# One turn of a 16-batch attention loop laid anew: the order of work on five engines in an adaLN block with linear attention and eight experts

## The reference, cut to what matters

```
h = layernorm(x) * (1 + ca) + sa
q, k = feature_map(h @ Wq.T + bq), feature_map(h @ Wk.T + bk)    # 16 heads, 8 -> 32 features
v = h @ Wv.T + bv
buf = [k.T @ v, sum(k)]
out = (q @ buf)[..., :-1] / (q @ buf)[..., -1:]
x = x + ga * (out @ Wo.T + bo)
h = layernorm(x) * (1 + cb) + sb
x = x + gb * (W2[e](gelu(W1[e](h) + b1[e])) + b2[e]),  e = argmax(h @ gate_W + gate_b)
```

## Time and profile before

| | us |
|---|---|
| median of 3 runs | 383.06 |
| lowest and highest run | 382.57, 385.99 |
| span of the profiled execution | 360.6 |
| what lies around it (median less span) | 22.5 |
| PE busy | 338.8 (94% of the span) |
| DVE, ACT, POOL busy | 271.2, 265.1, 213.2 |
| first part, to the first block's transpose | 0 to 211.4 |
| second part | 211.4 to 360.6 |

### The profile page before, as it was taken

How to read it: one execution, slowest core, us unless ns; L and a number is a source line. 1 busy time by engine, 2 the same in 40 slices (tenths; PEclk the granted TensorE clock), 3 DMA queues, 4 the chain that set the end, 5 groups by cost and what they waited for, 6 DMA issues and landing times.

```text
span 360.6 us, 13729 instructions
## 1 busy us (share of the span) xinstructions
PE 338.8 (94%) x4823; PEld 263.9 (73%) x4823; DVE 271.2 (75%) x1104; ACT 265.1 (74%) x644; POOL 213.2 (59%) x262
## 2 busy tenths in 40 slices
PE   6899999899988999998999999999999999999994
PEld 5445765566465566646665669999989999999993
DVE  3456997898879789878887978887677676666653
ACT  2688988799878888977888756676656667666761
POOL 3142386776667757857854618846767455545554
PEclk9999999999999999999999999999999999999999
DMA  7174656774566547444432467445657665545410
GB/s 233 50 253 166 210 184 221 259 243 160 177 227 205 176 167 230 163 132 156 153 133 100 149 163 227 142 118 150 194 161 269 209 184 147 147 128 135 137 38 12
DMA packets 40211, 60.47 MB, mean 168 GB/s; under 512 B 5426, under 2 KB 28086, under 8 KB 40016
## 3 DMA queue, kind: packets, MB, share of 16 engines
q1 hardware_dynamic: 33776, 42.54, 39.9%
q0 software_dynamic: 6368, 17.05, 12.5%
HBM read 28.63 MB, written 19.34 MB: 133 GB/s over the span
## 4 chain that ended last, share of the span: by engine, by line
PE 60%; ACT 15%; DMA 10%; DVE 6%; issue 5%; POOL 1%; SPq 1%; DVEq 1%; POOLq 0%; ACTq 0%
PE ps_proj L1350 16%; PE ps_feat L1337 9%; DMA qmix<-qsqs 9%; PE ps_proj L1132 6%; PE ps_den_gate L1337 4%; PE ps_proj L1182 4%; PE ps_kv L1337 4%; ACT qf L627 3%; ACT qvals L606 2%; ACT shared L588 2%; PE ps_kv L1198 2%; PE ps_out L1330 2%; ACT den L656 2%; ACT shared L581 2%; ACT kvm L600 2%
## 5 line engine op out<-in xcount | busy, mean ns | idle before, releaser
L545 POOL DMA_INDIRECT out<-kf,modb x71 | 70.1, 987 | 52.4 <-DVE kf L1060 47.0
L507 POOL DMA_INDIRECT experts_lists<-pay,slot x64 | 65.9, 1030 | 43.4 <-DVE slot L893 29.5
L1350 PE MATMUL ps_proj<-w2sb,qf 128*128 x568 | 75.0, 275 | 0.4 <-ACT qf L690 0.4
L1350 PEld LDWEIGHTS ps_proj<-w2sb,qf 128*128 128x128 f32 x568 | 68.9, 192 | 0.6 <-issue 0.6
L681 ACT ACTIVATE xT<-ps_out 128x128 f32<-128x128 f32 x71 | 19.7, 277 | 44.8 <-PE ps_out L1330 44.1
L1055 DVE TENSOR_TENSOR kf<-ps_proj,firsts_sb 128x128 f32<-128x128 f32 x71 | 20.7, 291 | 34.6 <-PE ps_proj L1350 22.6
L690 ACT ACTIVATE qf<-ps_feat,shared 128x128 f32<-128x128 f32 x144 | 40.9, 374 | 0.0
L1337 PE MATMUL ps_feat<-xT,shared 128*128 128x128 f32 x288 | 38.8, 277 | 1.5 <-issue 0.9
L1337 PEld LDWEIGHTS ps_feat<-xT,shared 128*128 128x128 f32 x288 | 35.0, 192 | 2.8 <-issue 1.7
L1132 PE MATMUL ps_proj<-shared,wsb 128*128 128x512 f32 x62 | 33.3, 620 | 1.0 <-ACT shared L581 0.4
L977 DVE COPY shared<-firsts_sb 128x516 f32 x71 | 31.4, 442 | 1.6 <-issue 1.5
(11 more groups left out here) (189 smaller groups left out, 890.3 us busy)
## 6 DMA issues: line engine op xcount, KB each, us to landing
modb<-experts_lists SPq DMA_DIRECT2D x71, 196.0 KB, 2.8
xall<-in_x SPq DMA_DIRECT2D x16, 256.0 KB, 3.0
pay<-modb SPq DMA_DIRECT2D x16, 256.0 KB, 3.0
qmix<-qvals SPq DMA_DIRECT2D x30, 128.0 KB
qmix<-qsqs SPq DMA_DIRECT2D x30, 128.0 KB
modb<-modulation_rows SPq DMA_DIRECT2D x4, 768.0 KB, 5.2
firsts_sb<-in_firsts SPq DMA_DIRECT2D x8, 322.0 KB, 4.2
w2sb<-in_w SPq DMA_DIRECT2D x8, 256.0 KB
```

The lines of the kernel that those rows point to most:

```text
L507: g_.indirect_dma_start(out=lists, in_=pay[b.home][:, t, :], in_offset=None, out_offset=bass.IndirectOffsetOnAxis(ap=slot[b.home][:, t:t + ...
L545: g_.indirect_dma_start(out=rows_out, in_=yb[u], in_offset=None, out_offset=bass.IndirectOffsetOnAxis(ap=token, axis=0), bounds_check=last ...
L1350: ins = mm(Y[u % 2][:, 0:D], g[u % R4][:, c * P:(c + 1) * P], w2sb[:, bass.ds(e * DFF + c * D, D)], start=(c == 0), stop=(c == FC - 1))
```

## The change

The arithmetic is the same; no instruction is added or taken away in a full turn, only order, banks and waits change. Part by part:

- project_k(b+1) stands in PE's turn right behind out_project(b-1) and writes bank G (the bank of the denominator) instead of PJ[0]; it waits until attention(b-1) has read G. k_values and k_squares of b+1 move forward with it on ACT.
- transpose_xn(b+1) stands ahead of out_project(b-1), modulate(b+1) between the two k_pairs, and project_v(b+1) and v_values(b+1) are done in turn b instead of b+1.
- normalise1(b+2) is done by DVE in turn b, behind kv_values, instead of normalise1(b+1) at the turn's head; POOL's rstd1_of goes ahead of rstd2_of.
- ACT makes q_squares(b+1) ahead of the logarithm of batch b instead of behind it.
- On PE gate and gate_transpose go behind kv_product, rank between denominator and numerator.
- On DVE centre_h2(b-1) goes ahead of kv_values(b), slots(b-2) behind scale_h2(b-1), directly ahead of attention(b).
- The single semaphore of the projections becomes three, and the first and the last turn have functions of their own.

```
 # POOL
+                if ahead and b.par == 0:
+                    rstd1_of(b.half + 3, b=b + 2)
                 if not first:
                     rstd2_of(b + -1, rows_of=None if second else b + -2)
-                if ahead and b.par == 0:
-                    rstd1_of(b.half + 3, b=b + 2)
                 if not first and not second:
                     scatter(b + -2, (0, 1))
                 gated(b, first)
 # ACT, the new turn
+                k_pair(b, 0)
+                modulate(b + 1)
+                k_pair(b, 1)
+                if not second:
+                    h2T_copy(b + -2)
+                k_values(b + 1)
+                k_squares(b + 1)
+                q_pair(b, 0)
+                if not second:
+                    gateT(b + -2)
+                q_pair(b, 1)
+                kvm_copy(b)
+                v_values(b + 1)
+                q_values(b + 1)
+                q_squares(b + 1)
+                rden_first(b)
                 if b.v + 2 < B:
                     normalise1(b + 2)
 # DVE
-                if not first and not last:
-                    normalise1(b + 1, lo=LT // 2)
                 if not first:
                     residual(b + -1)
                     second_stats(b + -1)
+                if not first and not last:
+                    centre_h2(b + -1)
...
+                kv_values(b, first)
...
+                if b.v + 2 < B:
+                    normalise1(b + 2, lo=LT // 2)
+                if not first and not second and not last:
                     experts(b + -2)
...
                 eps_values(b)
                 if not first and not last:
-                    centre_h2(b + -1)
                     scale_h2(b + -1)
+                if not first and not second and not last:
+                    slots(b + -2)
 # PE, the new turn
+                k_features(b)
+                if not second:
+                    transpose_h2(b + -2, first=b.v == 2)
+                transpose_xn(b + 1)
+                out_project(b + -1)
+                project_k(b + 1)
+                q_features(b)
+                kv_product(b)
+                if not second:
+                    gate(b + -2)
+                project_v(b + 1)
+                kv_transpose(b)
+                if not second:
+                    gate_transpose(b + -2)
+                project_q(b + 1)
+                eps_and_den(b)
+                if not second:
+                    rank(b + -2, first=b.v == 2)
+                numerator(b)
```

More of the change, by code:

```diff
@@ L277, in build @@
         s_bo = sem("bo_row_ready")
[L278 removed]
+        s_pk = sem("k_projected")
+        s_pq = sem("q_projected")
+        s_pv = sem("v_projected")
         s_kst = sem("k_parts")
@@ L635, in gateT, with rden_first @@
                 a.activation(lgT[:], I[:, 0:P], ACT.Copy).then_inc(s_lgT, 1)
[L637 to L653 removed]
+            def rden_first(b):
                 act.wait_ge(s_den, b.v + 1)
@@ L1278, in batch @@
             def batch(b, first=False, second=False, last=False, ahead=True):
-                third = b.v == 2
+                if first:
+                    return first_batch(b)
                 if last:
-                    count(0)
-                k_features(b, first)
-                if not first and not second:
-                    transpose_h2(b + -2, first=third)
-                v_project(b, last)
-                if not first:
-                    out_project(b + -1)
-                if not first and not second:
+                    return last_batch(b)
@@ L1289, in batch @@
+                k_features(b)
+                if not second:
+                    transpose_h2(b + -2, first=b.v == 2)
+                transpose_xn(b + 1)
+                out_project(b + -1)
+                project_k(b + 1)
+                q_features(b)
+                kv_product(b)
+                if not second:
                     gate(b + -2)
-                q_features(b, first)
-                if not first and not second:
+                project_v(b + 1)
+                kv_transpose(b)
@@ L1292, in batch @@
+                if not second:
                     gate_transpose(b + -2)
-                if not last:
-                    transpose_xn(b + 1)
-                else:
-                    table_transpose(0)
-                kv_product(b, first)
-                if not last:
-                    project(b + 1, 0)
-                if not first and not second and not last:
-                    rank(b + -2, first=third)
-                if last:
-                    keep_busy(10, H)
-                kv_transpose(b, first)
@@ L1305, in batch @@
-                if not last:
-                    project(b + 1, 1)
-                else:
-                    keep_busy(14, H)
-                attend(b)
-                if last:
-                    rank(b + -2)
+                project_q(b + 1)
+                eps_and_den(b)
+                if not second:
+                    rank(b + -2, first=b.v == 2)
+                numerator(b)
             pe.wait_ge(s_fw, 3)
@@ L1318, in _ @@
             mm(KV[0:B, 0:3 * D], sc, wmod_sb[:, 0:3 * D], start=True, stop=True)
-            project(start, 0, first=True)
-            project(start, 1, first=True, bank=I)
+            project_k(start)
+            project_q(start, bank=I)
             mm(G[0:B, 0:3 * D], sc, wmod_sb[:, 3 * D:6 * D], start=True, stop=True).then_inc(s_modp, 1)
```

157 lines of the change are left out of this document (96 added, 61 removed).

## The result

The changed kernel takes 401.74 us (median of 4 runs, 399.65 to 406.74), the kernel before beside it 384.52 (382.57 to 386.57): ratio 1.0453, interval 1.038 to 1.0527. Slower, as forecast; 399 was named, in a range of 388 to 405. One of the four runs, the one of 406.74, shows a lower granted clock than the others (0.973 against 0.980 to 0.986), and the ratio leaves it out. The profiled execution has a span of 400.4 and its own time is 402.22, so 1.8 us lie around its span, and not the 22.5 that the prediction added.

What follows compares the result with a forecast made beforehand. The kernel before was taken as bound by PE plus a DMA wait, the changed one by POOL's scatters and wo. 360.6 + 14.3 + 1.0 + 1.0 = 376.9 us of span, with 22.5 around it 399; range 388 to 405.

Steps and rivals of the forecast that it cites:

- the DMA wait: PE's q_features waiting for the DMA interleaving q's squares: counted as gone, 5.2 us over eight turns, some 8 over the loop.
- odd turn: Loop: slots ends at 9.67, then two scatters and wo end last, so a turn takes 13.02 us instead of 12.5.
- even turn: Turns 4, 6, 8, 10, 12: experts waits behind normalise1 for POOL's late rstd1_of, 1.50 us more, 14.52 in all.
- start: Batch 0: denominator and logarithm come later, out_project(0) by 1.3 us, 0.3 regained in turn 1: +1.0, between 0 and 1.5.
- end and second part: SP's first block load waits for batch 12's later last scatter: +1.0 us, between -0.8 and +1.8; second part unchanged.
- around the span: Outside the profiled execution: 22.5 us added to take the span to the runs' median.
- rival D: Loop: a further wait, scatters slower beside attention or a clock fall to 1.2 GHz; 405 us and more; chance 0.05.
- the clock holds: PE in the loop: despite idling 1.2 us in odd and 2.7 in even turns, the granted clock is not halved.
- port rule: POOL's scatters beside DVE: by the skill page an estimated 5 us more per turn, by the rows nothing; rows' price kept.
- A: Loop: POOL's path does not decide, PE and DVE up to oT do; turns of 11.9, ending at 375.5 us; chance 0.09.
- B: Loop: rstd1_of comes in time, so even turns equal odd ones, 13 turns of 13.02; 392 us; chance 0.12.
- E: Loop: POOL takes what the DMA wait gives, so turns stay 12.5; 383 to 385 us; chance 0.04.

Runs made afterwards that it cites:

- normalise1 late: The changed kernel with DVE's half of normalise1 of two batches on moved behind experts and the epsilon copy: 380.17 us, ratio 1.0505.
- two moves: The changed kernel with gated ahead of the first two scatters on POOL and, in even turns, normalise1's half behind slots on DVE: 378.5 us, ratio 1.0469.
- the squares moved: The kernel before with the squares of q ahead of the logarithm on ACT: 388.93 us, ratio 1.0145.
- slots late: The kernel before with slots behind scale_h2 on DVE, directly ahead of attention: 409.5 us, ratio 1.0708.
- four moves: The changed kernel with gated ahead of the scatters, slots ahead of scale_h2, even-turn normalise1 half behind slots, PE's gate ahead of kv_product: 413.12 us, ratio 1.0799.
- slots early: The changed kernel with slots ahead of scale_h2 on DVE: 373.3 us, ratio 1.0276.
- rstd2_of first: The changed kernel with gated ahead of the scatters, even-turn normalise1 half behind slots, and rstd2_of back ahead of rstd1_of on POOL: 366.0 us, ratio 1.0088.
- gated first: The changed kernel with gated (wo and the bias sum) ahead of the first two scatters on POOL: 373.43 us, ratio 1.0279.

## Why the prediction was right, and where it was not

**Direction and mechanism: right.** POOL's path from slots over two scatters to wo ends last, the DMA wait is gone (it came back in two turns each of the versions with gated and with slots moved, 0.75 to 2.37 us) and pays nothing, even turns are longer for the late shift. That holds in every full turn on chip 1. On chip 2, where the times of the result come from, wo ends last in 7 of the 13 turns alone. On chip 1, where the rows came from, the span was forecast as 376.9 and is 376.9. That agreement is partly luck, as the terms show (from the four windows):

| term | forecast | measured on chip 1 |
|---|---|---|
| odd turn | 13.02 | 12.6 to 12.7 (turn 9: 13.1; turn 14: 13.17) |
| even turn | 14.52 | 14.18 to 14.23 |
| loop, 13 turns | +14.3 | +10.4 |
| start | +1.0 | +1.2 |
| end and second part | +1.0 | +3.4 (in other traces of this order +1.5 to +1.6) and +1.1 |
| around the span | 22.5 | 1.8 |

*The odd turn* (turn 5). The gate's transpose was read at 5.87 (forecast 5.89), experts took 1.23 (1.22, though the two times named beside it, 118.58 to 119.89, are 1.31 apart). scale_h2 stands 1.06 in front of slots, not 1.30: the 1.30 was read from one turn in which it ran beside POOL's work, as did the 1.34 of its busy time; alone it has 1.14. From the end of slots to wo are 2.68, not 2.83, and from there to out_project 0.61, not 0.52. Together 0.34 less in this turn and 3.7 less over the thirteen (173.1 against 176.8). In turns 9 and 14 the first scatter starts 0.76 behind slots instead of 0.29; why, is open.

*The even turn.* The factors are there at 6.83 (forecast 6.80), experts begins at 7.38 (7.39; the terms written out, 6.80 and 0.53, give 7.33, and 0.06 goes unnamed). The 1.50 between the two kinds of turn came out as 1.5. This was the boldest number in the forecast and the best, for it was walked out on POOL instruction by instruction.

*The end* was undersized for this trace. The last scatter of batch 12 starts 3.12 behind out_project(14), as forecast (3.2). SP's next write of gate rows waits until that scatter has landed, and it stands ahead of the first block's load in both kernels; it comes 4.71 behind the scatter, where the kernel before has 2.59. I had kept the same 3.5 for both. That scatter on POOL and the two issues of SP, kernel before and then changed kernel, chip 1:

```profile
203.98 0.96 POOL L507 DMA_INDIRECT experts_lists<-pay,slot  x1 [0.30 <-issue]
...
206.57 0.62 SPq L381 DMA_DIRECT2D pay<-modb  x1
208.88 9.21 SPq L432 DMA_DIRECT2D modb<-experts_lists  x9
```

```profile
217.09 0.96 POOL L516 DMA_INDIRECT experts_lists<-pay,slot  x1 [0.30 <-issue]
...
221.80 0.62 SPq L386 DMA_DIRECT2D pay<-modb  x1
223.97 9.81 SPq L437 DMA_DIRECT2D modb<-experts_lists  x9
```

Behind out_project(14) the first load is issued after 6.54 in the one and 10.00 in the other. But 4.71 stands in this trace alone. In the two traces of the changed kernel on chip 2 it is 2.93 and 2.94, with normalise1 late on chip 1 2.90, and there the end costs 1.5 to 1.6 more than in the kernel before, not 3.4. What differs here is in the trace's DMA packets: the last four of the scatter's queue start at 220.36 and later, 0.83 behind the rest, while a 16 KB packet of an instruction queue is in flight from 219.39 to 220.37. That this packet held them up is likely by the times and not shown. With the usual landing the forecast for the end was sound and the span would have been some 1.8 shorter, so the agreement of 376.9 with 376.9 owes that much to an accident. PE waits for the load:

```profile
226.49 0.45 PE L1404 MATMUL ps_out<-csb,modb 128*128 128x128 f32 x1 [3.56 <-DMA modb<-experts_lists]
```

Behind that idle stretch the granted clock was 0.5 (the 1.2 GHz level) for 6.8 us, from 225.5 to 232.3, and the second part took 1.1 more. Where the clock stayed at 1.00 there, with gated or slots moved, it took 148.2 and 147.7. In the loop of this trace the clock stayed at 1.00 with PE busy in 156 of 173 us, as the row-based side of the prediction had it. In others it didn't. In the profile of the result itself it fell in turn 9, which took 15.41, behind a stretch in which PE was busy 5.29 of 7.00 us:

```profile
139.60:143.00 3.40, 3.40 (x26) 0.52 (x28) 2.64 (x13) 2.30 (x5) 2.98 (x4) 0.51 0.35 124
```

The second trace of the changed kernel on chip 2 has one such turn of 15.80, and on chip 1 the version with normalise1 late has one and the one with two moves has two. So a part of rival D is in the result after all, in one turn and not in each, and "the clock holds" was too strong. The rule of the Trainium skill (TensorE: Matmul & The Clock Gate, Part 1), that low activity halves the clock, agrees with these falls.

*Around the span.* The wrong step was to take "median less span" as something of the kernel. It was 1.8 and the difference between two kinds of chips. The forecast time still fell only 2.7 from the measured one, because both kernels were timed on the same kind of chip, and the cost was 17.2 us there and 16.1 to 16.6 on chip 1. That is luck in part, since on chip 2 it is made of other turns, as follows.

**The other kind of chip.** In the profile after of the result the alternation is not 13.0 and 14.5: from batch 2 on the turns are 13.28, 13.87, 13.53, 14.56, 13.47, 14.95, 13.08, 15.41, 14.18, 14.47, 13.47, 14.44, 13.45, the even ones mostly the shorter. There wo ends last in the even turns from 4 on, in turn 9 and in no other odd one; in those PE comes late, behind a slow k_features. PE's rows at the end of one of them:

```profile
121.79 0.35 PE L1202 MATMUL ps_proj<-feat_w,shared 32*128 32x128 f32 x1 [0.46 <-issue]
121.81 0.48 PE L1205 MATMUL ps_feat<-csb,shared 32*128 32x128 f32 x3
122.54 0.36 PE L1205 MATMUL ps_feat<-csb,shared 32*128 32x128 f32 x1 [0.25 <-issue]
122.55 0.48 PE L1205 MATMUL ps_proj<-csb,shared 32*128 32x128 f32 x3
123.27 0.26 PE L1205 MATMUL ps_proj<-csb,shared 32*128 32x128 f32 x1 [0.24 <-issue]
```

It had begun at 119.49 and ran smoothly until 121.06; then PE stops again and again, 0.24 to 0.46 us each time, in the midst of matmuls that wait for nothing. k_features took 3.97 where chip 1 shows 2.0 in the same order of work. And the waits of that profile name a releaser that none of the nine traces of chip 1 has (the one shown ahead of the prediction among them) and that all five of chip 2 have:

```profile
ACT kf L629 <- remote: 22.6, 7, 4.0
```

What it stands for, the profile doesn't say. The clock row reads 1.00 beside it. The second part takes 166.9 there against 150.4. What holds PE up on chip 2 stays open. In the traces of chip 2 k_features was slow (3.8 to 4.4 until ACT's first exponential) in the changed kernel, where attention and the scatters run beside it, 2.3 to 3.6 in the kernel before with the squares moved, 2.13 in the kernel before with slots late until its last turn (4.05), and 2.13 in every turn of the version with four moves. So the kind of chip is not enough for it; the order of work has a share. On chip 1 no version shows more than 2.2, but for two turns with normalise1 late (2.41 and 2.58) and three with slots early (2.29, 2.29 and 2.96). No experiment separated the cause.

**The port rule.** The prediction weighed the rule of the Trainium skill (SBUF — State Buffer, section Who interferes with whom) for scatters only and kept the rows' price. For the scatters that was right: 0.96 to 1.23 in every turn beside attention, nothing near the estimated 5 us. The same section's lock, one of DVE and POOL shut out until the other's instruction ends, did show where the prediction had not looked, on DVE's side, wherever DVE's own SBUF work fell beside POOL's long sum: 1.55 instead of 0.59 (rstd2_of first), 1.22 instead of 0.17 (gated first), 0.97 instead of 0.17 (two moves), each ending 0.02 to 0.09 behind POOL's instruction. Here page and trace agree on who waits and until when. No run took the sum away to show it as the cause; that the same DVE instructions have their usual length wherever nothing of gated runs beside them speaks for it.

**The rivals.** A (11.9 a turn) is what odd turns do once gated goes first, 11.85, so its price was right and its condition false: POOL's order does decide. B (even turns like odd ones) is nearly what the version with normalise1 late shows, 13.2 and 13.76, and it was worth nothing, for the cover it gives up. D came in one turn of the result, by the clock. E missed.

## What to carry to other kernels

An engine that is busy 60% of its time can still set the pace: ask what stands between the value that it waits for and the value that others want from it, and walk that stretch instruction by instruction, in odd and even turns apart. Before adding "what lies around the span" to a sum, see that the timed runs and the profile come from the same kind of chip; a re-profiled kernel before is the cheapest experiment there is. And when a long POOL instruction is moved out of the way of one wait, look at what DVE does at its new time, for the two can stand in each other's way for as long as it lasts.

## What the runs showed of the hardware

Two kinds of chips ran the same program 21 us apart (362.3 and 383.4 for the kernel before); of the 23.5 us between two spans of the changed kernel (376.9 and 400.4) 16.5 are in the second part. PE stalled inside one run of matmuls for which the profile names no wait (0.24 to 0.46 us every few of them) with a granted clock of 1.00. The granted clock fell to 0.5 for 3.4 us at a time inside the loop in six of the fourteen traces; in the two of them on chip 1 such a turn took 1.4 to 1.7 us more. A sum over 8 columns on DVE took 0.97 instead of 0.17, another instruction over 4 columns 1.22 instead of 0.17, and a normalisation of two tiles 1.55 instead of 0.59, beside a 128x512 sum of POOL, each ending within 0.1 us of it. A scatter took from 2.59 to 4.71 us from its start to the step that waited for it on SP, and 2.59 to 3.24 but for the one.
